# Attention and mixture block on one core: ten maxima ahead of the first scores, transposes of maxima inside a run, the values' bias behind the first split

## The chip, the cores and the metric

The kernel runs on one core of one Trainium2 chip. The metric is the device time of one execution in microseconds; the median of the runs counts. Of the core's engines, TensorE (PE) does the matmuls, VectorE (DVE), ScalarE (ACT) and GpSimd (POOL) the rest, and SyncE (SP) issues the transfers. The engines run beside each other and meet only at semaphores.

## What is computed

The input is x of 2 x 64 x 32 x 32 in f32, that is two batches of 1024 tokens with 64 channels. Cut to what matters:

```python
def _L0_conv_ref(x, ...):                 # softmax attention, 8 heads of 8 channels, then group norm
    q, k, v = proj(Wq, bq), proj(Wk, bk), proj(Wv, bv)
    attn = softmax(einsum('bhnd,bhmd->bhnm', q, k) * scale)
    out  = einsum('bhnm,bhmd->bhnd', attn, v) -> @ Wo.T + bo -> group norm -> + x
x = _L0_conv_ref(x, ...)
t = _to_tokens(x)
t = t + _L1_attn_ref(_ln_t(t), v_matrix, q_matrix)   # 4 layers of 8 linear heads (no softmax)
t = t + _L1_ffn_ref(_ln_t(t), ...)                   # top 2 of 8 experts
```

The change touches only the softmax attention. Everything behind it is the tail.

## The kernel before

**Tiling.** The attention is cut into 16 blocks (batch, pair of heads, half of the queries), each of 8 units (tiles of 128 keys), so there are 128 units. Two units make a run: 64 runs, four to a block. For a unit there are scores (keys on the partitions, 512 queries, for two heads h = 0 and 1: two matmuls of 64 rows), the exp of them on ACT into `probs`, and the values: 8 matmuls that add into one bank over the 8 units of a block. An exp wants the maximum of its query subtracted. So for each block there are also 8 maxima: for 128 queries and one head all 1024 scores are computed once more with the queries on the partitions (two matmuls of 512 columns, `max_half(v, 0)` and `max_half(v, 1)`), and DVE reduces them to one column of `negmax` (L1069). Maximum number v belongs to block v // 8. When a block's eight are out, GpSimd splits them into two parts (for the precision of the f32r matmuls), TensorE turns them into rows, ACT copies these out of PSUM, and they become two more rows of the queries' operand `qop`, so that the scores matmul subtracts the maximum by itself. For blocks 0 and 1 the turning is `rows_of_max` (four matmuls, L464, and two copies by ACT straight into `qop`); for the others it is `maxima_to_rows` (one transpose, L477, called max_t in ST_JOBS), a copy by ACT (L927) and two transfers on SP's queue (`max_rows`, L327).

**Who waits for whom.** The maxima use PSUM banks 0 to 3, two at a time: maximum v waits on `slot_free` until DVE is done with v - 2. Scores, output transposes, max_t and the second batch's projections share a ring of banks 4, 5 and 6 in the order of ST_JOBS, and ACT empties them in the same order. When there are no maxima any more, a unit's two scores take a pair of banks and one exp of 1024 (kind `unit`); these runs are called wide here. Scores of h = 0 and a maximum of h = 1 use different halves of TensorE's rows and run at the same time, which is why the maxima are put between the scores.

**The lead.** Before the first scores, TensorE issues LEAD = 10 maxima. Between them stand the projection for queries and keys of batch 0 in two halves of tokens (`queries_and_keys`, ahead of maxima 2 and 3), the eight tiles of the values' projection, two ahead of each of maxima 4 to 7 (`v_tiles`), and fills behind maxima 7 and 8 (8 small matmuls on zeros each, nothing of the result). The projection goes through ACT and GpSimd (`part`, signalled by `parts0_in` and `parts0`), is stored to DRAM by SP and loaded back as the operands of blocks 2 to 7, ten transfers for each slot. Then comes `rows_of_max(0)`.

**The runs.** `max_jobs(g)` gives the maxima that run g issues: two, but four for the runs in CATCH_UP = (0, 1). So run 0 issues 10 to 13, run 1 14 to 17, run 2 18 and 19, and run 56 the last; units from 114 on are wide. A run with maxima goes: scores, maximum, values(first unit of the run before), maximum, scores, [two more maxima], [rows_of_max(1) in run 2], [output transposes of a block, in run 4k+1], [max_t, also in run 4k+1, for block k+1], values(second unit of the run before). Run 0 has the two projections of batch 1 ahead of its maxima 12 and 13.

**GpSimd's queue** in this part: zeros for the operands, part and split for batch 0, the last copy of q (`rep_pool`, which maximum 8 waits for), the bias of the values (`v_ready`, which values(0) waits for), then for each block the split of its maxima; behind that of block 1 the parts of batch 1 and the zeros of its operands; from block 3 on one `normalize` a block.

## Time and profile before

| | us |
|---|---|
| median of 3 runs | 276.4 |
| lowest, highest | 276.04, 278.12 |
| the profiled execution | 275.98 |
| its span in the profile | 274.2 |

The profile shows one execution. Its span is the time from the first to the last instruction; 1.8 us lie around it. Times in the rows are counted from the span's start. A line number names the line of the kernel that issued an instruction. TensorE's matmuls overlap each other at their ends, so the start of the next instruction is the better measure of what one costs than its own length; the chain view shows the lengths cut in that way.

### The profile page before, as it was taken

How to read it: one execution, taken by the hardware profiler on the slowest of the kernel's cores; microseconds unless marked ns; L12 is line 12 of the kernel's file. 1: busy time of each engine (PE TensorE's matmuls, PEld its weight loads, DVE VectorE, ACT ScalarE, POOL GpSimd, SP SyncE). 2: the span in 40 equal slices, each digit the busy share in tenths (PEclk: the TensorE clock that was granted, in tenths of full speed). 3: DMA queues.
4: the chain of work that ended last, by engine and by line, in shares of the span. 5: the costliest groups of instructions: out<-in, count | busy, mean ns of one | idle time of the engine just before them, and what ended most of it. 6: DMA issues, size and time to landing. Idle time of an engine off the chain costs nothing.

```text
span 274.2 us, 5520 instructions
## 1 busy us (share of the span) xinstructions
PE 253.5 (92%) x2078; PEld 115.3 (42%) x2078; DVE 196.0 (71%) x283; ACT 177.2 (65%) x360; POOL 47.1 (17%) x83
## 2 busy tenths in 40 slices
PE   8999899999999999999999999998986998789895
PEld 6364333333333333333333333332433785558421
DVE  2896566898898898988988989987004662338752
ACT  2725436888897888888888878889792122118720
POOL 7961088110000100000103001000000000000251
PEclk9997757999999999999999999999999999999999
DMA  4046100062122121440100000000000000000002
GB/s 125 0 163 131 22 0 2 15 218 67 40 77 54 29 81 33 99 157 14 68 4 1 1 5 2 1 4 0 5 1 0 2 0 2 0 0 2 1 0 77
DMA packets 6050, 10.30 MB, mean 38 GB/s; under 512 B 2032, under 2 KB 3664, under 8 KB 5896
## 3 DMA queue, kind: packets, MB, share of 16 engines
q1 hardware_dynamic: 6024, 9.95, 12.5%
q8 instruction: 16, 0.26, 0.4%
q14 instruction: 10, 0.08, 0.1%
HBM read 7.10 MB, written 2.62 MB: 35 GB/s over the span
## 4 chain that ended last, share of the span: by engine, by line
PE 77%; DVE 9%; ACT 6%; issue 4%; POOL 1%; DMA 1%; DVEq 0%; SPq 0%; ACTq 0%
PE psum L511 26%; PE psum L418 16%; PE psum L453 15%; ACT probs L915 3%; PE psum L734 3%; PE psum L389 2%; PE psum L643 2%; ACT probs L911 1%; PE psum L477 1%; PE psum L652 1%; DVE negmax L1069 1%; PE psum L715 1%; PE psum L395 1%; PE psum L531 1%; DMA wqk_sb<-in_wqk 1%
## 5 line engine op out<-in xcount | busy, mean ns | idle before, releaser
L1069 DVE TENSOR_REDUCE negmax<-psum 128x1 f32<-128x1024 f32 x128 | 155.2, 1224 | 25.0 <-PE psum L418 22.0
L915 ACT ACTIVATE probs<-psum 128x512 f32<-128x512 f32 x228 | 124.0, 598 | 30.1 <-PE psum L453 24.4
L418 PE MATMUL psum<-kop,qop 64*128 64x512 f32 x256 | 95.1, 460 | 1.7 <-DVE negmax L1069 1.3
L453 PE MATMUL psum<-qop,kop 64*128 64x512 f32 x256 | 90.5, 453 | 0.4 <-DVE negmax L1069 0.3
L511 PE MATMUL psum<-probs,v_aug 128*32 128x256 f32 x1024 | 82.1, 398 | 1.4 <-ACT probs L911 0.3
L418 PEld LDWEIGHTS psum<-kop,qop 64*128 64x128 f32 x256 | 38.6, 192 | 32.9 <-DVE negmax L1069 16.8
L453 PEld LDWEIGHTS psum<-qop,kop 64*128 64x128 f32 x256 | 36.9, 189 | 28.2 <-ACT probs L915 11.1
L511 PEld LDWEIGHTS psum<-probs,v_aug 128*32 128x32 f32 x1024 | 21.4, 109 | 44.8 <-ACT probs L915 30.8
L813 POOL TENSOR_TENSOR attn<-o_tok,rden 128x64 f32<-128x64 f32 x15 | 4.4, 295 | 113.8 <-DVE rden L1060 113.8
L867 POOL TENSOR_TENSOR early<-probs,early 128x512 f32<-128x512 f32 x5 | 6.3, 1269 | 59.6 <-ACT probs L1006 59.5
L521 PE MATMUL psum<-cbf_sb 128*128 128x256 bf16 x124 | 14.8, 272 | 0.0
L911 ACT ACTIVATE probs<-psum 128x1024 f32<-128x1024 f32 x14 | 13.4, 1048 | 1.2 <-PE psum L453 1.2
L521 PEld LDWEIGHTS psum<-cbf_sb 128*128 128x128 bf16 x124 | 12.2, 100 | 1.4
L1060 DVE RECIPROCAL rden<-o_tok 128x8 f32<-128x8 f32 x15 | 2.9, 195 | 11.4 <-ACT o_tok L934 11.4
L1253 DVE TENSOR_TENSOR early<-psum,early 128x512 f32<-128x512 f32 x11 | 7.1, 687 | 4.6 <-PE psum L715 4.6
L734 PE MATMUL psum<-early,expw_sb 128*64 128x512 f32 x32 | 8.2, 610 | 0.5 <-POOL early L867 0.5
L484 PE MATMUL psum<-consts_sb,o_sb 128*128 128x128 f32 x32 | 6.9, 298 | 0.8 <-ACT o_sb L904 0.8
L837 POOL CAST max_part<-negmax 128x8 fp32r<-128x8 f32 x14 | 2.7, 190 | 28.4 <-DVE negmax L1069 28.4
L1006 ACT ACTIVATE probs<-psum 128x512 f32<-128x512 f32 x5 | 3.0, 597 | 6.3 <-PE psum L715 6.2
L477 PE MATMUL psum<-consts_sb,max_part 128*16 128x128 f32 x14 | 3.8, 269 | 3.5 <-ACT probs L915 2.4
L904 ACT ACTIVATE o_sb<-psum 128x256 f32<-128x256 f32 x16 | 6.3, 395 | 0.8 <-PE psum L511 0.8
L389 PE MATMUL psum<-x_sb,wqk_sb 128*128 128x512 f32 x8 | 6.4, 893 | 0.0
(177 smaller groups left out, 199.2 us busy)
## 6 DMA issues: line engine op xcount, KB each, us to landing
parts_scratch<-early SPq DMA_DIRECT2D x4, 512.0 KB, 3.4
qop<-parts_scratch SPq DMA_DIRECT2D x28, 64.0 KB
vt_sb<-in_vt SPq DMA_DIRECT2D x1, 1024.0 KB, 5.0
kop<-parts_scratch SPq DMA_DIRECT2D x14, 64.0 KB
kop<-parts_scratch SPq DMA_DIRECT2D x28, 32.0 KB
x_sb<-in_x SPq DMA_DIRECT2D x2, 256.0 KB, 2.8
q_pair<-in_q_pairs SPq DMA_DIRECT2D x1, 512.0 KB, 3.3
qop<-max_row SPq DMA_DIRECT2D x28, 4.0 KB
```

What stands on the lines that cost most here:

```text
L389: return nc.tensor.matmul(psum[:, bank, :], wqk_sb[:, b, :], x_sb[:, hf * NH:(hf + 1) * NH], start=True, stop=True)
L418: last = nc.tensor.matmul(psum[:, 2 * (v % 2) + c, :], qop[at, b * PP + pp, qh * NH + t * P:qh * NH + (t + 1) * P], kop[at, b * PP + pp, c ...
L453: last = nc.tensor.matmul(psum[:, bank, :], kop[at, b * PP + pp, mt * P:(mt + 1) * P], qop[at, b * PP + pp, qh * NH:(qh + 1) * NH], start= ...
L477: nc.tensor.transpose(psum[0:SPLIT * 2 * HT, bank, 0:P], max_part[:, blk % 2, :, :, :].rearrange("p h s t -> p (h s t)"), ident).then_inc( ...
L484: last = nc.tensor.transpose(psum[:, bank, q * P:(q + 1) * P], o_sb[:, blk % 2, q * P:(q + 1) * P], ident)
L511: last = nc.tensor.matmul(psum[j * VW:(j + 1) * VW, PV_BANK, 0:QB].rearrange("p (x n) -> p x n", x=2), v_aug[:, mt, b, 2 * pp + h, :], pro ...
L521: nc.tensor.matmul(psum[:, bank, 0:WARM_COLS], ident_bf, cbf_sb[:, 1:1 + WARM_COLS // P, :], start=True, stop=True, skip_group_check=True)
L734: nc.tensor.matmul(psum[b * C:(b + 1) * C, MOE_BANKS[c], :], expw_sb[:, k, :], scaled[:, r % SCALED, :], start=False, stop=k == E // 2 - 1 ...
L911: last = nc.scalar.activation(probs[:, n % P_RING, :, :], psum[:, bank:bank + 2, :], ACT.Exp, scale=SCALE)
L915: last = nc.scalar.activation(probs[:, n % P_RING, h, :], psum[:, bank, :], ACT.Exp, scale=SCALE)
L1069: V.tensor_reduce(negmax[:, i, h * HT + t:h * HT + t + 1], psum[:, bank:bank + 2, :].rearrange("p a n -> p (a n)"), AX_X, ALU.max, negate= ...
L1253: V.tensor_tensor(scaled[:, i % SCALED, :], psum[:, GB_BANKS[i % len(GB_BANKS)], :], yt2[:, b, c * NH:(c + 1) * NH], ALU.mult).then_inc(S[ ...
```

## The change

- CATCH_UP is (0,): only run 0 issues four maxima. Run 1 issues 14 and 15, run 2 16 and 17, run 57 the last; units from 116 on are wide.
- In the lead, the first projection stays ahead of maximum 2, together with tile 0 of the values; the second is done in two halves of 256 tokens ahead of maxima 3 and 4; the other tiles stand as V_TILES says (two ahead of maxima 5, 6 and 7, one ahead of 8). There is one fill, behind maximum 8, instead of two.
- max_t of block k+1 moves from behind the scores and output transposes of run 4k+1 to the middle of run 4k+2, behind values(first) and between its two pairs of scores; in a wide run behind its scores.
- The values' bias on GpSimd stands behind the split of block 0 instead of ahead of it.
- The order of the two additional maxima of a doubled run other than run 0 falls away with the run.

```diff
-CATCH_UP = (0, 1)
-FILL_FROM = 7
+CATCH_UP = (0,)
+V_TILES = {2: (0, 1), 5: (1, 3), 6: (3, 5), 7: (5, 7), 8: (7, 8)}
...
-            blk = (g + 3) // RUNS_OF
-            return blk if (g + 3) % RUNS_OF == 0 and DIRECT <= blk <= LAST else None
+            blk = (g + 2) // RUNS_OF
+            return blk if (g + 2) % RUNS_OF == 0 and DIRECT <= blk <= LAST else None
...
             if max_jobs(g):
-                ST_JOBS += [("scores", u, h) for u, h in scores_of(g)]
+                ST_JOBS += [("scores", u, h) for u, h in scores_of(g)[:TOGETHER]]
+                if block_of_rows(g) is not None:
+                    ST_JOBS.append(("max_t", block_of_rows(g), 0))
+                ST_JOBS += [("scores", u, h) for u, h in scores_of(g)[TOGETHER:]]
             else:
                 ST_JOBS += [("unit", u, 0) for u in range(TOGETHER * g, TOGETHER * (g + 1))]
+                if block_of_rows(g) is not None:
+                    ST_JOBS.append(("max_t", block_of_rows(g), 0))
...
-            if block_of_rows(g) is not None:
-                ST_JOBS.append(("max_t", block_of_rows(g), 0))
...
+            def half_queries_and_keys(hf, c):
+
+                return nc.tensor.matmul(psum[:, 4 + hf, c * QB:(c + 1) * QB], wqk_sb[:, 0, :],
+                                        x_sb[:, hf * NH + c * QB:hf * NH + (c + 1) * QB], start=True, stop=True,
+                                        skip_group_check=True)
...
             for v in range(LEAD):
-                if v in (2, 3):
-                    hf = v - 2
-                    pe.wait_ge(S["rep_dve"], hf + 1)
-                    queries_and_keys(0, hf, 4 + hf).then_inc(S["qk_full"], 1)
-                elif 4 <= v < 8:
-                    if v == 4:
-                        pe.wait_ge(S["in_v"], 16)
-                        pe.wait_ge(S["rep_dve"], 3)
-                    elif v == 6:
-                        pe.wait_ge(S["rep_act"], len(CHUNKS) + 1)
-                    v_tiles(2 * (v - 4))
+                if v == 2:
+                    pe.wait_ge(S["rep_dve"], 1)
+                    queries_and_keys(0, 0, 4).then_inc(S["qk_full"], 1)
+                    pe.wait_ge(S["in_v"], 16)
+                    pe.wait_ge(S["rep_dve"], 3)
+                elif v == 3:
+                    half_queries_and_keys(1, 0)
+                elif v == 4:
+                    half_queries_and_keys(1, 1).then_inc(S["qk_full"], 1)
+                elif v == 6:
+                    pe.wait_ge(S["rep_act"], len(CHUNKS) + 1)
+                if v in V_TILES:
+                    v_tiles(*V_TILES[v])
                 for c in range(HALVES):
                     max_half(v, c)
-                if v == FILL_FROM:
+                if v == LEAD - 2:
                     pe.wait_ge(S["parts0_in"], 2 * HALVES)
-                if FILL_FROM <= v < LEAD - 1:
                     fill()
             rows_of_max(0)
...
                     if g:
                         values(TOGETHER * (g - 1))
+                    if block_of_rows(g) is not None:
+                        maxima_to_rows(block_of_rows(g))
                     max_half(jobs[1], 0)
...
                     for u, h in s:
                         scores(u, h)
+                    if block_of_rows(g) is not None:
+                        maxima_to_rows(block_of_rows(g))
...
-                if block_of_rows(g) is not None:
-                    maxima_to_rows(block_of_rows(g))
...
-            pool.wait_ge(S["v_out"], 2)
-            pool.wait_ge(S["in_bv"], 16)
-            v_at = v_aug[:, :, :, :, 0:DH].rearrange("p t b h d -> p t (b h) d")
-            nc.gpsimd.tensor_tensor(v_at, v_at,
...
                 pool.wait_ge(S["max_split"], blk + 1)
+                if blk == 0:
+                    pool.wait_ge(S["v_out"], 2)
+                    pool.wait_ge(S["in_bv"], 16)
+                    v_at = v_aug[:, :, :, :, 0:DH].rearrange("p t b h d -> p t (b h) d")
+                    nc.gpsimd.tensor_tensor(v_at, v_at,
+                                            bv_sb[:].rearrange("p (o h d) -> p o h d", o=1, d=DH).broadcast_to([P, TT, B * H, DH]),
+                                            ALU.add).then_inc(S["v_ready"], 1)
+                    pool.wait_ge(S["v_ready"], 1)
```

## Rows read from the trace of the kernel before

**Rows 1.** The page, busy time, share of the span and instructions of each engine.

```profile
PE 253.5 (92%) x2078; PEld 115.3 (42%) x2078; DVE 196.0 (71%) x283; ACT 177.2 (65%) x360; POOL 47.1 (17%) x83
```

**Rows 2.** Stretches: length, busy us (instructions) by engine, granted clock, DMA share, GB/s.

```profile
24.50:31.20 6.70, 6.70 (x11) 2.43 (x12) 2.33 (x2) 2.66 (x5) 0.00 (x0) 0.50 0.46 78
31.20:34.80 3.60, 2.47 (x17) 0.86 (x14) 3.35 (x3) 2.17 (x4) 0.00 (x0) 0.97 0.00 0
34.80:44.90 10.10, 9.90 (x53) 3.95 (x55) 6.01 (x6) 4.43 (x8) 9.35 (x8) 0.50 0.00 0
...
46.05:189.27 143.22, 139.77 (x1316) 52.35 (x1312) 129.28 (x120) 120.47 (x252) 11.57 (x45) 1.00 0.16 46
189.27:205.50 16.23, 13.72 (x157) 5.76 (x153) 1.16 (x3) 14.50 (x20) 0.98 (x4) 1.00 0.01 3
```

**Rows 3.** Chain that ended last: start us, us, what; the lead.

```profile
1.18 2.45 DMA wqk_sb<-in_wqk
...
11.88 1.06 PE psum L389 x2
...
13.59 0.64 PE psum L395 x4
14.23 0.66 PE psum L418 x2
...
18.85 2.35 POOL v_aug L786
...
23.14 0.74 PE psum L453 x2
```

**Rows 4.** Timeline, lead: start, us, engine, line, operation, count, idle before and releaser.

```profile
13.63 8.86 DVE L1069 TENSOR_REDUCE negmax<-psum 128x1 f32<-128x1024 f32 x7 [0.28 <-PE psum L418]
...
18.73 0.62 PE L471 MATMUL psum<-idle 128*128 128x128 bf16 x8
...
21.80 0.66 PE L464 MATMUL psum<-ident_r,max_wide 128*128 128x128 f32 x4 [0.58 <-POOL max_wide L830]
```

**Rows 5.** Timeline from run 1 to the start of run 5.

```profile
31.45 3.49 DVE L1069 TENSOR_REDUCE negmax<-psum 128x1 f32<-128x1024 f32 x3 [1.93 <-PE psum L418]
...
35.06 0.20 POOL L829 CAST max_wide<-negmax 128x8 fp32r<-128x8 f32 x1 [13.31 <-DVE negmax L1069]
...
37.16 0.79 PE L453 MATMUL psum<-qop,kop 64*128 64x512 f32 x1
...
43.22 3.51 POOL L771 MEMSET kop<- 128x4096 uint32 x1
...
46.05 0.49 PE L453 MATMUL psum<-qop,kop 64*128 64x512 f32 x1
...
48.51 0.50 PE L453 MATMUL psum<-qop,kop 64*128 64x512 f32 x1
```

**Rows 6.** Timeline of a steady run 4k+1, from its start to max_t.

```profile
80.98 0.50 PE L453 MATMUL psum<-qop,kop 64*128 64x512 f32 x1
...
82.07 0.20 POOL L838 TENSOR_TENSOR max_part<-negmax,max_part 128x8 fp32r<-128x8 f32 x1
...
83.02 0.44 PE L484 MATMUL psum<-consts_sb,o_sb 128*128 128x128 f32 x2
...
83.65 0.27 PE L477 MATMUL psum<-consts_sb,max_part 128*16 128x128 f32 x1 [0.19 <-ACT probs L915]
```

**Rows 7.** Timeline of the wide runs, from the last max_t to the last exps.

```profile
192.04 0.27 PE L477 MATMUL psum<-consts_sb,max_part 128*16 128x128 f32 x1 [1.09 <-ACT o_tok L934]
...
192.64 1.27 SPq L327 DMA_DIRECT2D qop<-max_row  x2
...
193.79 5.61 ACT L911 ACTIVATE probs<-psum 128x1024 f32<-128x1024 f32 x6 [1.17 <-PE psum L453]
...
196.57 0.73 PE L453 MATMUL psum<-qop,kop 64*128 64x512 f32 x4
...
201.70 3.77 ACT L911 ACTIVATE probs<-psum 128x1024 f32<-128x1024 f32 x4
```

More of the change, by code:

```diff
@@ L390, in queries_and_keys, with v_tiles @@
                                         start=True, stop=True)
-            def v_tiles(first):
-                c = first // 4
-                for t in range(first, first + 2):
-                    last = nc.tensor.matmul(psum[:, 6 + c, (t % 4) * P:(t % 4 + 1) * P], x_sb[:, t * P:(t + 1) * P],
+            def half_queries_and_keys(hf, c):
+                return nc.tensor.matmul(psum[:, 4 + hf, c * QB:(c + 1) * QB], wqk_sb[:, 0, :],
+                                        x_sb[:, hf * NH + c * QB:hf * NH + (c + 1) * QB], start=True, stop=True,
+                                        skip_group_check=True)
+            def v_tiles(first, end):
+                for t in range(first, end):
+                    last = nc.tensor.matmul(psum[:, 6 + t // 4, (t % 4) * P:(t % 4 + 1) * P], x_sb[:, t * P:(t + 1) * P],
                                             wv_sb[:], start=True, stop=True, skip_group_check=True)
-                if first % 4 == 2:
-                    last.then_inc(S["v_full"], 1)
+                    if t % 4 == 3:
+                        last.then_inc(S["v_full"], 1)
             def max_half(v, c):
@@ L573, in _ @@
                     scores(*s[3])
-                    if g == 0:
-                        for hf, v in enumerate(jobs[2:]):
+                    for hf, v in enumerate(jobs[2:]):
+                        if g == 0:
                             pe.wait_ge(S["in_wqk1"], 16)
                             queries_and_keys(1, hf, st_free(("qk", hf, 0))).then_inc(S["st_full"], 1)
-                            for c in range(HALVES):
-                                max_half(v, c)
-                    else:
                         for c in range(HALVES):
-                            for v in jobs[2:]:
-                                max_half(v, c)
+                            max_half(v, c)
                 else:
```

3 lines of the change are left out of this document (removed).

## Prediction

> **What bounds the kernel now.** I read the page first: TensorE is busy for 92% of the span [rows 1], so it is the first suspect, but a busy share does not tell the pace. So next the stretches, each with its granted clock [rows 2]. From 24.5 to 31.2 us and from 34.8 to 44.9 us the granted clock is 0.50, that is 1.2 instead of 2.4 GHz: 16.8 us at half pace, at the very place where the change works. From 46.05 to 189.27 the clock is 1.00 and TensorE is busy 139.8 of 143.2 us; DVE (129.3) and ACT (120.5) are behind it: the middle is TensorE's. Behind it ACT leads, 14.50 us of 16.23.
>
> Then the chain and the timeline. In the lead TensorE's work stands back to back until it waits for GpSimd [rows 3]: the values' bias takes 2.35 us from 18.85, and the split of the first maxima stands behind it, though its eight maxima are out at 13.63 + 5 x 1.27 = 19.98 (seven reduces in 8.86 [rows 4]; the eighth maximum is the fifth of them). Only the split's end lets rows_of_max(0) go, at 21.80; the first scores start at 23.14. Run 1 is next [rows 5]: it issues four maxima, its TensorE waits for DVE (three reduces in 3.49 us from 31.45; 2.47 us of matmuls in 3.6 us [rows 2]), the clock falls behind it, and run 2 starts only at 37.16. A run at full clock takes 48.51 - 46.05 = 2.46 us; runs 2 and 3 with rows_of_max(1) take 8.89 us, up to 46.05. In the steady part a block of four runs takes 143.22/53 x 4 = 10.81 us. Four times 2.46 is 9.84; the output's transposes take about 0.33 (two of the 0.16 that each of L395's takes), max_t 0.2 of its 0.27, and 0.4 is waiting. Most of it is seen: the output transposes start at 83.02 and are through at 83.35, but max_t starts at 83.65, 0.30 later, since ACT still reads the bank that is next in the ring [rows 6]. The other 0.1 is the wait for o_copied.
>
> **The lead.** The matmuls before rows_of_max(0) stay (two halves of the second projection cost what one whole did) but for one fill: 8 matmuls, 0.62 long, 0.55 to the next instruction. TensorE's contiguous stretch up to 21.22 (21.80 - 0.58 [rows 4]) ends 0.55 earlier, at 20.65. The split now needs maximum 7 alone. In the new order its matmuls end at 18.4 (half a projection less stands ahead of it, and tile 7 behind it), DVE is done at 19.7, and 0.6 us as now (21.80 - 21.20) makes 20.3, before TensorE asks. So rows_of_max(0) starts at 20.6 and the first scores at 21.9, 1.2 us earlier. The bias on GpSimd ends at 22.7; the first to need it is values(0), at 27.8. It hides behind run 0, with 5 us to spare; without that cover it would cost up to 2.35. The second half of the parts reaches GpSimd some 1 us later, and q's last copy, which queues behind it, ends at 18.0, before maximum 8 wants it at 18.7. On SP's queue the store and the operands behind it go 1 us later. Block 2's operands are asked for at 29.8 instead of about 35 us; they are the first of two slots whose ten loads each SP issues from about 21 on, so they should land by 26. I cost all of this at nothing.
>
> **Runs 0 to 3.** If the clock stays up, run 0 goes from 21.9: four scores and maximum 11 until 23.7, then two projections of 1.06 and two maxima of 0.66 [rows 3]: 27.15. Run 1 is an ordinary run, 2.46 and 0.1 for DVE, so run 2 starts at 29.75 instead of 37.16. Runs 2 and 3 with 0.66 for rows_of_max(1) take 5.6: run 4 starts at 35.35 instead of 46.05. That is 10.7 us: 1.2 from the lead, 3 to 4 from two maxima and DVE's waits in run 1, the rest from the clock. Does it stay up? It fell at 24.5 behind 0.58 us of waiting at rows_of_max [rows 4] and lone matmuls on half the rows, and at 34.8 behind a stretch with 1.1 us of idle TensorE [rows 2]. Both go: the wait is gone, the projections move forward into that stretch, and run 1 has no maxima without a scores partner. Against it, the lead loses a fill.
>
> The Trainium skill ("TensorE: Matmul & The Clock Gate", section "A second HAM failure mode: psum-queue depth-cycling") says that frequent short idle times between groups of matmuls are enough to make the gate swing; the fall at 24.5 behind a longest wait of 0.58 us agrees. Its section "HAM oscillation — how this bites in real kernels" blames long waits between bursts; by that alone the clock would never fall in the new kernel. By this second rule the sum stays as it is; by the first, case two of the rivals becomes the likelier one, 265.6.
>
> **A new wait.** GpSimd's work behind the split of block 1 (parts and zeros) runs from 35.06 to 46.73 [rows 5], 11.7 us. Now it starts at 30.8 and ends at 42.5; block 2's split behind it on that queue ends at 43.0. The transpose of these maxima stands in the middle of run 6, at 35.35 + 2 x 2.46 + 0.4 + 1.23 = 41.9. TensorE waits 1.1 us, once, and all its maxima and scores with it.
>
> **The steady part.** max_t moves from behind run 4k+1 into run 4k+2, behind values, and its maxima one run later too. There the ring of three gives it a bank whose scores were read long before, and the scores behind it need exps that end 0.1 us or more ahead. So the 0.30 goes and the 0.2 of work stays. Is the split there? It ends at 82.27, 1.29 into the run that starts at 80.98 [rows 6]; moved by a run whose end holds the output's transposes it is 0.96 into run 4k+2, and TensorE asks at 1.23. 13 blocks x 0.30 = 3.9 us. The other bound is nothing: the 0.30 comes back at another bank. The rows leave later: ACT copies them until 1.85 into the run, SP's second issue starts at 2.5, and run 4k+4 needs them at 5.1, 2.6 later. A landing is not shown. At most it is 3.3 us (the second issue of block 15 starts at 192.64 + 0.64, and the scores at 196.57 don't wait [rows 7]), at least nothing; at 3.3 it costs 0.7 a block. I take the 2.45 of wqk's 64 KB [rows 3], the nearest transfer that the chain shows, so it costs nothing. "DMA: Bandwidth & Descriptors", section "Anatomy of one DMA", in the Trainium skill gives a fixed cost of about 2.0 us; by that there is no wait either.
>
> **The end.** One more run has maxima, one fewer is wide. Run 57 starts at 189.27 - 10.7 + 1.1 - 3.9 = 175.8 and takes 2.46 + 0.4 = 2.9: run 58 at 178.7. The wait of 1.09 us for ACT's copy of the output, which stood here, is gone [rows 7]. But block 15's rows are now copied behind the exps of units 116 and 117, their second issue starts 3.1 into run 58, and they land at about 5.3, where ACT runs dry at 4.3: 1.3 us with the scores' own 0.33. ACT's last twelve exps with two copies took 193.79 to 205.47, 11.7; with 0.4 to start, 0.3 for the row's copy and 1.3 of waiting it is 13.7, to 192.4. The tail behind it is the same work.
>
> **Sum:** 10.7 + 3.9 - 1.1 - 0.4 (16.6 instead of 16.2 from run 57 on) = 13.1 us. The profiled execution took 275.98 (span 274.2 and 1.8 around it), 0.4 under the runs' median of 276.4. 275.98 - 13.1 = 262.9; against the median 263.3.
>
> **Rivals.**
> - *The clock stays up, the sum holds:* 263.3. Chance 0.5.
> - *The clock still falls in runs 0 to 6,* from the thinner lead or the wait of 1.1 us. One low stretch of 6.7 us as now [rows 2] costs 3.4 us, but then GpSimd's wait is hidden: 263.3 + 3.4 - 1.1 = 265.6. Both stretches as now: 16.8/2 - 1.1 = 7.3 on top, 270.6. Chance 0.25.
> - *The moved transpose gives nothing,* its 0.30 coming back as a wait for a bank that ACT holds: 263.3 + 3.9 = 267.2. For it, ACT's share; against it, the ring. Chance 0.12.
> - *The rows land late,* at the bound of 3.3: 0.7 for 13 blocks and 1.0 at the end: 273.4. Chance 0.08.
> - *Slower:* the same place, a landing beyond that. 13.1 us are spent at 0.94 a block of 14, a landing 3.5 us behind the issue; over 1% slower (2.8 us more) from 3.7, at 279. The bound is from the last block, when no other transfer was on the queue; that is all that speaks for it. Chance 0.03. The last 0.02 are for a change that moves nothing: 276.
>
> **How the numbers follow.** The likeliest is 263.3. Below it, the assumed waits of 1.3 at the end and 1.1 at run 6 could be absent: 261. Above, the range takes in one fall of the clock, the 0.30 unmoved, and parts of both: 269.5. Beyond it lie two falls and late rows, under 2 in 10. About 1%, 2.8 us, is what a measurement here can tell from no change. Faster by over 1%: all but the last two cases, 0.95; same 0.02; slower 0.03.
>
> **What would show it.** rows_of_max(0) at about 20.6, the first scores at 21.9; the clock at 1.00 from 20 to 45 us; run 2 at 29.8, run 4 at 35.4; one idle of some 1 us on TensorE ahead of the first max_t; 13 blocks of 10.5 us, with no idle before max_t; no wait for the rows' DMA except ahead of unit 120. It is wrong if the clock row still has its fives there, or if a block stays at 10.8.

## The result, and the profile after

The changed kernel took 264.14 us in the median of four executions (263.63 to 264.78), the kernel before 276.57 beside it (276.04 to 278.12): a ratio of 0.954, with an interval of 0.950 to 0.959. The profiled execution took 264.78, its span is 263.0. The kernel before varies with the clock that it is granted: in the 49 further executions shown below it took 270.6 to 280.05 us, 21 of them over 275, so the 12.4 us of this comparison are not the same thing as what the change is worth in general. That is most of what the experiments are about.

The page of the kernel after: busy time by engine, and TensorE's granted clock in 40 slices.

```profile
span 263.0 us, 5508 instructions
...
PE 245.6 (93%) x2071; PEld 114.5 (44%) x2072; DVE 195.9 (74%) x283; ACT 178.4 (68%) x362; POOL 47.1 (18%) x83
...
PEclk9999999999999999999999999999999999999999
```

TensorE's busy time fell by 7.9 us from the 253.5 of [rows 1], while it issued only seven instructions fewer (the eight of a fill are gone, one more for the second projection in halves). DVE and ACT have nearly the same busy time as before. So most of what TensorE lost is not work but work at half pace: the clock row has no slice below 9 any more, and this answers to the two stretches at 0.50 in [rows 2].

Stretches of the kernel after (length, busy us and instructions by engine, granted clock, DMA share, GB/s), from TensorE's lead to the end of the attention:

```profile
10.90:21.71 10.81, 10.81 (x48) 5.94 (x47) 10.51 (x9) 3.76 (x7) 6.58 (x7) 1.00 0.26 102
...
22.00:29.80 7.80, 7.38 (x34) 3.32 (x35) 6.15 (x6) 5.70 (x10) 1.73 (x1) 1.00 0.56 127
29.80:35.40 5.60, 5.60 (x54) 2.42 (x55) 4.98 (x5) 4.86 (x9) 3.06 (x6) 1.00 0.10 14
35.40:178.70 143.30, 141.26 (x1332) 54.62 (x1333) 131.62 (x122) 123.80 (x258) 18.77 (x47) 1.00 0.16 46
178.70:192.40 13.70, 12.02 (x133) 5.03 (x129) 2.53 (x4) 11.93 (x19) 1.26 (x5) 1.00 0.01 3
```

**The lead.** Everything in this profile stands 1.01 us later than in the one of before: DVE's first reduce starts at 10.88 and not 9.87. The reason is in the chain that ended last; the second row is for the end.

```profile
4.47 2.05 PE psum L386 x2
...
183.95 1.71 DMA qop<-max_row
```

The first f32 matmuls took 2.05 us for two. In the execution of before the same ones took 1.12 (its timeline; the second row is the six matmuls behind them):

```profile
4.38 1.12 PE L383 MATMUL psum<-x_sb,w_rep 128*128 128x512 f32 x2
...
5.71 2.82 PE L383 MATMUL psum<-x_sb,w_rep 128*128 128x512 f32 x6
```

So in the profile after they ran at about half pace, at a place that the change does not touch. The first record of the clock in the trace is its rise, at 6.37 us here and at 3.99 in the profile of before; ahead of that record the view of stretches shows 1.00 all the same. Times of this profile are therefore lowered by 1.0 below where they are set against the prediction.

The timeline of the lead (start, us, engine, line, operation, count, idle time before and its releaser):

```profile
20.82 0.20 POOL L830 CAST max_wide<-negmax 128x8 fp32r<-128x8 f32 x1 [2.02 <-DVE negmax L1078]
...
21.38 2.35 POOL L845 TENSOR_TENSOR v_aug<-v_aug,bv_sb 128x1024 f32<-128x1024 f32 x1
...
21.71 0.66 PE L473 MATMUL psum<-ident_r,max_wide 128*128 128x128 f32 x4
...
23.04 0.73 PE L462 MATMUL psum<-qop,kop 64*128 64x512 f32 x2
```

The split of the first maxima no longer waits for the bias; it is over at 21.30, and rows_of_max(0) starts at 21.71 without the 0.58 of idle time of [rows 4]. Less 1.0 that is 20.7, and the first scores are at 22.0. The bias runs behind the split and holds nobody up.

**Runs 2 to 6.** The timeline of TensorE and GpSimd; the first two rows are the starts of run 2 and run 4.

```profile
30.87 0.49 PE L462 MATMUL psum<-qop,kop 64*128 64x512 f32 x1
...
36.62 0.50 PE L462 MATMUL psum<-qop,kop 64*128 64x512 f32 x1
...
40.17 3.51 POOL L779 MEMSET kop<- 128x4096 uint32 x1
...
43.74 0.19 POOL L838 CAST max_part<-negmax 128x8 fp32r<-128x8 f32 x1
...
44.27 0.28 PE L486 MATMUL psum<-consts_sb,max_part 128*16 128x128 f32 x1 [0.90 <-POOL max_part L839]
```

Run 4 starts at 35.6 on the clock of before, where [rows 5] has 46.05. The price is in the last row: the zeros for the operands occupy GpSimd until 43.7, the split of block 2's maxima stands behind them, and TensorE, done with values at 43.30, waits for it until 44.27, 0.97 us (0.90 in the bracket, the rest is the overlap of matmuls).

**A steady block.** The rows are the starts of two runs 4k+1, a block apart, and between them the output's transposes, the split, max_t and what follows it, and the two transfers of the rows.

```profile
71.80 0.50 PE L462 MATMUL psum<-qop,kop 64*128 64x512 f32 x1
...
73.85 0.44 PE L493 MATMUL psum<-consts_sb,o_sb 128*128 128x128 f32 x2
...
74.22 0.64 PE L520 MATMUL psum<-probs,v_aug 128*32 128x256 f32 x8
...
75.51 0.20 POOL L839 TENSOR_TENSOR max_part<-negmax,max_part 128x8 fp32r<-128x8 f32 x1
...
76.02 0.28 PE L486 MATMUL psum<-consts_sb,max_part 128*16 128x128 f32 x1
76.23 0.49 PE L427 MATMUL psum<-kop,qop 64*128 64x512 f32 x1
...
76.63 1.28 SPq L330 DMA_DIRECT2D qop<-max_row  x2
...
82.39 0.50 PE L462 MATMUL psum<-qop,kop 64*128 64x512 f32 x1
```

A block takes 82.39 - 71.80 = 10.59 us, where the prediction worked out 10.81 for before. max_t has no idle time in front of it; the 0.30 between the output's transposes and max_t in [rows 6] is gone. The split is over at 75.71, 0.3 ahead of max_t.

**The end.** The wide runs: the rows' transfers of the last block, the wait for them, and the last exps.

```profile
183.30 1.26 SPq L330 DMA_DIRECT2D qop<-max_row  x2
...
185.71 0.73 PE L462 MATMUL psum<-qop,kop 64*128 64x512 f32 x4 [1.14 <-DMA qop<-max_row]
...
190.48 3.77 ACT L920 ACTIVATE probs<-psum 128x1024 f32<-128x1024 f32 x4
```

The second transfer is issued at 183.93, and the scores of unit 120 start at 185.71, held by it. The last exps end at 194.25. Run 57 starts at 177.67, so this part takes 16.6 us, as forecast; the wait of 1.09 for the copy of the output in [rows 7] is exchanged for one of 1.14 for the rows.

### The profile page after: what moved, and what is told of

It is laid out like the page before. It is cut to its first block, busy times and chain, and to the rows that moved or that the text cites. A ratio compares the mean times of both kernels' runs of the same rounds, so it can differ in the third digit from the quotient of the medians.

```text
span 263.0 us, 5508 instructions
## 1 busy us (share of the span) xinstructions
PE 245.6 (93%) x2071; PEld 114.5 (44%) x2072; DVE 195.9 (74%) x283; ACT 178.4 (68%) x362; POOL 47.1 (18%) x83
## 4 chain that ended last, share of the span: by engine, by line
PE 76%; DVE 9%; POOL 5%; issue 4%; ACT 3%; DMA 2%; SPq 0%; DVEq 0%; ACTq 0%; POOLq 0%
PE psum L520 23%; PE psum L427 16%; PE psum L462 14%; PE psum L742 3%; PE psum L493 2%; PE psum L651 2%; PE psum L660 1%; POOL qop L779 1%; POOL kop L779 1%; DVE negmax L1078 1%; ACT probs L920 1%; PE psum L392 1%; PE psum L723 1%; PE psum L486 1%; POOL early L857 1%
## 5 line engine op out<-in xcount | busy, mean ns | idle before, releaser
L924 ACT ACTIVATE probs<-psum 128x512 f32<-128x512 f32 x232 | 126.0, 598 | 19.9 <-PE psum L462 15.7
L427 PE MATMUL psum<-kop,qop 64*128 64x512 f32 x256 | 92.7, 444 | 0.6 <-DVE negmax L1078 0.3
L462 PE MATMUL psum<-qop,kop 64*128 64x512 f32 x256 | 89.6, 445 | 1.2 <-DMA qop<-max_row 1.1
L520 PE MATMUL psum<-probs,v_aug 128*32 128x256 f32 x1024 | 80.5, 390 | 1.5 <-ACT probs L920 0.3
L427 PEld LDWEIGHTS psum<-kop,qop 64*128 64x128 f32 x256 | 37.6, 184 | 24.5 <-DVE negmax L1078 13.0
L920 ACT ACTIVATE probs<-psum 128x1024 f32<-128x1024 f32 x12 | 11.6, 1030 | 1.5 <-PE psum L462 1.3
L1015 ACT ACTIVATE probs<-psum 128x512 f32<-128x512 f32 x5 | 3.0, 597 | 6.3 <-PE psum L723 6.2
L889 ACT ACTIVATE early<-psum,rep_cols 128x512 fp32r<-128x512 f32 x4 | 2.9, 775 | 5.2 <-DVE rep_cols L1055 5.1
L779 POOL MEMSET qop<- 128x3072 uint32 (+1 forms) x2 | 6.2, 3086 | 0.1
```

The source lines that it names most:

```text
L427: last = nc.tensor.matmul(psum[:, 2 * (v % 2) + c, :], qop[at, b * PP + pp, qh * NH + t * P:qh * NH + (t + 1) * P], kop[at, b * PP + pp, c ...
L462: last = nc.tensor.matmul(psum[:, bank, :], kop[at, b * PP + pp, mt * P:(mt + 1) * P], qop[at, b * PP + pp, qh * NH:(qh + 1) * NH], start= ...
L520: last = nc.tensor.matmul(psum[j * VW:(j + 1) * VW, PV_BANK, 0:QB].rearrange("p (x n) -> p x n", x=2), v_aug[:, mt, b, 2 * pp + h, :], pro ...
L779: nc.gpsimd.memset(op[:, slots, :].bitcast(U32), 0).then_inc(S["padded"], 1)
L920: last = nc.scalar.activation(probs[:, n % P_RING, :, :], psum[:, bank:bank + 2, :], ACT.Exp, scale=SCALE)
L924: last = nc.scalar.activation(probs[:, n % P_RING, h, :], psum[:, bank, :], ACT.Exp, scale=SCALE)
```

## The experiments

**Two theories** stood against each other after this. *The schedule*: each part of the change takes its waits away, and the clock only follows, since in the old kernel it falls behind idle time on TensorE (the prediction's account). *The clock*: most of the gain is that the new order keeps the clock up, and whether it falls is not a matter of idle time. All kernels of one group ran on one chip beside the kernel before.

### The bias alone

The kernel before, with the bias of the values behind the split of block 0 and nothing else:

```diff
-            pool.wait_ge(S["v_out"], 2)
...
-            pool.wait_ge(S["v_ready"], 1)
             chain = [3]
...
                 pool.wait_ge(S["max_split"], blk + 1)
+                if blk == 0:
+                    pool.wait_ge(S["v_out"], 2)
...
+                    pool.wait_ge(S["v_ready"], 1)
```

> The kernel before with one edit: the values' bias stands behind the split of block 0 on GpSimd. Theory (as in the prediction, two causes for the early gain): rows_of_max(0) no longer waits 0.58 us, TensorE goes on at 21.2, first scores 0.6 us earlier; run 1 still issues four maxima and its clock dip stays; the first dip (24.5) may go, since the wait ahead of it is gone. Time 275.9 if both dips stay (-0.6), 272.5 to 273.5 if the first one goes (-0.6 and half of 6.7 us, less what DVE takes back in run 1). Rival: the bias alone carries the early gain: run 4 at 36 instead of 46, time 266 to 268.

Measured: 273.31 us in the median of ten (269.9 to 280.01), ratio 0.995 (0.989 to 1.000) to 25 executions of before with a median of 273.7 (270.68 to 279.29). Both kernels fall into groups by the clock of their whole span: before has nine at 270.7 to 271.2 with a clock of 0.992, and seven at 276.3 and more with 0.951 to 0.968; bias_only has four at 269.9 to 270.5 with 0.993, and four at 276.9 and more with 0.957. Among those with a high clock the part is worth 0.8 us, near the 0.58 that it removes.

The profiled execution is one of the long ones, 277.06. First its rows_of_max(0), from the timeline:

```profile
21.08 0.66 PE L464 MATMUL psum<-ident_r,max_wide 128*128 128x128 f32 x4
```

Then its stretches, ahead of rows_of_max(0) and behind 24.7 us:

```profile
10.00:21.08 11.08, 11.06 (x53) 5.87 (x53) 10.50 (x9) 3.72 (x6) 7.54 (x8) 1.00 0.28 106
...
24.70:45.00 20.30, 19.41 (x80) 7.39 (x78) 11.03 (x10) 8.35 (x15) 9.79 (x8) 0.50 0.14 26
```

The wait is gone, TensorE was busy for 11.06 of 11.08 us before it, and the clock falls all the same, at the same place, and stays down for 20.3 us. So the wait of 0.58 us was not what made it fall in [rows 2].

### One doubled run alone

```diff
-CATCH_UP = (0, 1)
+CATCH_UP = (0,)
```

> The kernel before with CATCH_UP = (0,) alone: maxima one run later, max_t stays at the end of run 4k+1. Theory: the split of a block then ends about 3.75 us into run 4k+1 while TensorE asks for it at 2.4, so each of 13 blocks waits 1.4 us instead of 0.3: +14 us, against 4 to 5 won in run 1: about 286, more (to 295) if the clock falls behind these waits. The moved transposes are then what the one doubled run needs. Rival: the doubled run is the gain and the transposes only go along: 268 to 270.

Measured: 305.39 us (305.21 to 308.8, four executions), ratio 1.124 (1.112 to 1.136): 34.5 us more than the best group of before (270.9), and worse than expected. TensorE's wait for the split, once in each block (in total, times, longest), and one place of it in the timeline:

```profile
PE psum L477 <- POOL max_part L838: 22.0, 14, 2.7
```

```profile
111.45 0.33 PE L477 MATMUL psum<-consts_sb,max_part 128*16 128x128 f32 x1 [1.48 <-POOL max_part L838]
...
111.71 1.08 PE L511 MATMUL psum<-probs,v_aug 128*32 128x256 f32 x8
```

Maxima that come one run later are split one run later, and a max_t at the end of run 4k+1 asks before the split is there: 22.0 us of idle TensorE in 14 places. Behind it the eight matmuls of values take 1.08 instead of 0.64 us: the clock has gone to its lower level, and it does so again and again (the whole span has 0.926). The waits are 22.0 us where the profile of before has 2.4, that is 19.6 of the excess. A clock of 0.926 over 303.5 us is 45 us at half pace, which can cost up to 22, and run 1 gives some 3 back; the parts were not taken apart further. The doubled run may only go together with the move of max_t.

The same profile shows one thing more, ahead of its first fall at 46.7 us:

```profile
24.00:46.00 22.00, 18.82 (x143) 7.76 (x143) 16.41 (x14) 16.16 (x32) 12.15 (x11) 1.00 0.17 31
```

This kernel has the old lead and the wait of 0.58 us at rows_of_max(0), at 22.34, and its TensorE is idle for 3.2 of these 22 us, and yet the clock stays at 1.00 in this execution.

### The kernel before, its idle places filled

Eight small matmuls on zeros ahead of rows_of_max(0), and 4, 5 and 12 of them in run 1 ahead of three of its maxima, in unused columns of the values' bank. In this first form they begin a new sum in that bank, and the result is off by 0.028, presumably because the values' sum of the first unit of block 0 is lost; in the second form, further below, it is not.

```diff
+            fill()
             rows_of_max(0)
...
+                    if g == 1:
+                        fill_beside(4)
                     max_half(jobs[1], 0)
...
                             for v in jobs[2:]:
+                                if c == 0:
+                                    fill_beside(5 if v == jobs[2] else 12)
                                 max_half(v, c)
```

> The kernel before with more small matmuls on zeros in the places where TensorE waits: 8 ahead of rows_of_max(0), and in run 1 4 ahead of maximum 15, 5 ahead of 16 and 12 ahead of 17 (into unused columns of the values' bank). No order and no dependency changes, so it measures the clock by itself. Theory: the granted clock stays at 1.00 from 20 to 45 us; run 0's two projections take 1.06 instead of 2.0 each, runs 2 and 3 take 5.6 instead of 8.9 us; 270 to 271.5. Rival 1: the waits, not the clock, are the time: 276.5 or a little more. Rival 2: the fills do not hold the clock: rows at 0.50 remain, 276 to 277.

Measured: 272.37 us (269.68 to 274.33, ten executions), ratio 0.999 (0.993 to 1.005), and none above 275, where 12 of the 25 of before were. Its profile (272.17 us), one stretch and the start of run 4:

```profile
14.00:52.00 38.00, 37.41 (x278) 17.93 (x278) 32.54 (x28) 23.89 (x45) 18.37 (x17) 1.00 0.24 69
```

```profile
40.77 0.49 PE L453 MATMUL psum<-qop,kop 64*128 64x512 f32 x1
```

The clock stays at 1.00 through both places where it fell, and run 4 starts 6.3 us earlier than in the profile of before (40.77, less 1.05 by which this profile is late, against 46.05). That is what the low clock had cost there. With a full clock the old schedule is still 39.7 - 35.6 = 4.1 us behind the changed one at run 4: this is the lead and run 1. The median lies 0.9 us above the range expected; the profiled execution has 1.05 us of it from its slow start.

### The changed kernel with the bias back ahead of the split

```diff
+            pool.wait_ge(S["v_out"], 2)
...
+            pool.wait_ge(S["v_ready"], 1)
             chain = [3]
...
-                if blk == 0:
-                    pool.wait_ge(S["v_out"], 2)
...
-                    pool.wait_ge(S["v_ready"], 1)
```

> The changed kernel with the bias back ahead of the first split. Theory: the bias can start only when the second half of the values is copied (about 20.0), so the split ends near 22.8 and rows_of_max(0) starts 1.1 us later: 265.2 with the clock at 1.00 throughout; if the wait of 1.1 us makes the clock fall once, another 2 to 3.4: 267 to 268.5. Rival: the cover is elsewhere and the bias costs nothing: 264.1.

Measured: 270.6 us (269.28 to 271.17, ten executions), 6.5 above the changed kernel, more than either figure expected. The wait, from the timeline, and the stretch with the low clock:

```profile
22.96 1.11 PE L473 MATMUL psum<-ident_r,max_wide 128*128 128x128 f32 x4 [1.78 <-POOL max_wide L838]
```

```profile
22.80:36.30 13.50, 13.34 (x40) 6.33 (x44) 6.03 (x5) 6.05 (x11) 0.11 (x1) 0.51 0.31 69
```

The wait is 1.78 us here and not 0.58, since the new order has the projections' tiles later and TensorE at rows_of_max earlier, while the bias takes its 2.33 us as before. Behind it 13.5 us run at a clock of 0.51, in all ten executions (their spans have 0.973 to 0.98). Run 2 starts at 36.79 where the changed kernel has 30.87, and this profile's lead is 0.6 earlier (DVE's first reduce at 10.26), so run 2 is 6.5 us late: 1.8 of waiting, and 4.7 of low clock. That is the whole difference. So this part, worth 0.8 us by itself in the old kernel, carries 6.5 in the new one.

### The second group: the lead, run 1, and the filled kernel without its fault

The changed kernel again first:

> The changed kernel as it is, beside the kernel before on the same chip. The kernel before spread from 270.7 to 279.3 us in the last job, with granted clocks of the whole span from 0.992 down to 0.951. Theory: the changed kernel has no place left where the clock falls, so it stays within 1.5 us around 264, and against the kernel before in its executions at clock 0.99 it wins 6.5 us, against the others up to 15. Rival: its clock falls in some executions too, and it spreads by 3 us and more.

Measured: 264.31 us (263.59, 263.87, 264.76, 266.66), ratio 0.974 (0.965 to 0.983) to 13 executions of before with a median of 272.81. The one of 266.66 is the profiled one. Its timeline has the reason, at the replicas of the projection:

```profile
6.87 4.57 PE L386 MATMUL psum<-x_sb,w_rep 128*128 128x512 f32 x6
```

The six took 2.82 us in the profile of before. Here they ran at about half pace; the first record of the clock in this trace is its rise at 10.40 us, and ahead of it the view shows 1.00.

Run 1 doubled again, with everything else as changed (run 56 is then the last with maxima):

```diff
-CATCH_UP = (0,)
+CATCH_UP = (0, 1)
...
+                        for c in range(HALVES):
+                            for v in jobs[2:]:
+                                max_half(v, c)
```

> The changed kernel with CATCH_UP = (0, 1) and the old order of the four maxima of run 1; lead, bias and max_t as changed. Theory: run 1 waits for DVE some 3 us, as in the kernel before; the clock falls behind it in part of the executions; at the end one wide run more and one ordinary run less give 0.4 back: 266.5 at clock 1.00, 268 to 271 where it falls. Rival: four maxima in run 1 are harmless once the lead is shorter: 264.

Measured: 266.31, 266.45, 269.16 and 271.01 us, with clocks of 0.993, 0.992, 0.981 and 0.974; ratio 0.984 (0.973 to 0.994). One of the waits for DVE in run 1, in the profile of the execution of 266.45, and the stretch behind them:

```profile
31.08 0.72 PE L427 MATMUL psum<-kop,qop 64*128 64x512 f32 x3 [0.64 <-DVE negmax L1082]
```

```profile
32.00:35.30 3.30, 3.30 (x22) 1.13 (x16) 3.12 (x3) 1.08 (x2) 3.08 (x4) 0.51 0.00 0
```

Counted from DVE's first reduce, so without the start, this profile is 3.9 us behind the changed kernel's at run 4 and 2.5 at its end: the rest comes back because the wait at the first max_t is gone and one run more is wide. The expected time at a clock of 1.00 was not seen, since even the best executions have a short low stretch; it is part of the 2.5.

The old order of the lead, with its two fills, in the changed kernel (the `for v in range(LEAD)` loop of before; the tiles two ahead of each of maxima 4 to 7):

```diff
-                if v == 2:
...
+                if v in (2, 3):
+                    hf = v - 2
+                    pe.wait_ge(S["rep_dve"], hf + 1)
+                    queries_and_keys(0, hf, 4 + hf).then_inc(S["qk_full"], 1)
...
-                if v == LEAD - 2:
+                if v == FILL_FROM:
                     pe.wait_ge(S["parts0_in"], 2 * HALVES)
+                if FILL_FROM <= v < LEAD - 1:
                     fill()
```

> The changed kernel with the lead's old order (two whole projections ahead of maxima 2 and 3, two tiles ahead of each of 4 to 7, two fills). Theory: maximum 7 ends later by half a projection less one tile, and one more fill stands in the contiguous stretch: rows_of_max(0) 0.55 us later, nothing else: 264.7, clock 1.00. Rival: the lead's new order is what keeps the clock up: a stretch at 0.50 and 267 or more.

Measured: 265.15, 266.8, 266.95 and 270.4 us with clocks of 0.998, 0.987, 0.987 and 0.981; ratio 0.980 (0.972 to 0.988). Stretches of the profile (270.4 us):

```profile
13.00:23.99 10.99, 10.97 (x52) 5.77 (x53) 10.40 (x9) 3.72 (x6) 5.01 (x7) 1.00 0.29 107
...
27.00:37.80 10.80, 10.72 (x37) 3.84 (x36) 5.61 (x5) 4.52 (x9) 0.15 (x1) 0.53 0.25 54
```

TensorE was busy for 10.97 of 10.99 us ahead of rows_of_max(0), which it reached without a wait and with one fill more than the changed kernel, and the clock fell at about 27.0. The changed kernel's own stretch is the first one above, 10.81 of 10.81, and there it stays up. The two hardly differ in how busy TensorE is, only in what it does when.

The schedule part is small. rows_of_max(0) starts at 23.99, that is 11.28 behind DVE's first reduce (12.71), where the changed kernel has 10.83: 0.45 us, near the 0.55 expected. At its end this execution is 3.8 us behind the changed kernel, counted in the same way, so about 3.4 are the low clock. The other 2.8 of its 270.4 us are a slow start, and for the executions without a profile the two cannot be told apart.

A rival is that the start decides whether the clock falls later. Two pairs of profiles speak against it. after_again started as late as this one (first reduce at 12.77) and its clock never fell; after_rows_at_end, further below, started as early as bias_only (9.72 and 9.80), and only bias_only's fell.

The filled kernel of before without its fault, the small matmuls adding to zero columns (`start=False`):

> The kernel before with small matmuls on zeros where TensorE waits, as in before_kept_busy, but adding into the unused columns instead of starting a new sum there (in before_kept_busy that start wiped the sum of unit 0's values; here the whole computation is kept). Theory: the same clock and time as there, 269.7 to 274.3, median 272.4, with run 2 at about 33.5 to 34.5 and run 4 at about 40 to 41: the executions above 275 of the kernel before are gone. Rival: the fills only shift the low stretches: the kernel before's spread to 279 is back.

Measured: 272.29 us in the median of ten (seven at 271.51 to 272.76, two at 274.0 and 274.11, one at 278.07), ratio 1.004 (1.000 to 1.008). With both forms, 1 execution of 20 is above 275, of before 21 of 49. So with the fills the clock stays up more often. What they cost isn't shown: this median is 1.3 us over the best group of before, but its profiled execution (272.16) starts 0.87 us later than the profile of before, and counted from the first reduce rows_of_max(0) stands at 11.93 in both. In its profile the clock falls elsewhere, behind the wait for ACT's copy of the output ahead of the last max_t:

```profile
186.00:191.00 5.00, 4.27 (x37) 1.68 (x37) 0.20 (x1) 2.50 (x5) 0.29 (x1) 0.66 0.03 7
```

### The third group: the place of max_t, and a version beyond

The changed kernel with max_t at the end of run 4k+2 instead of its middle (and ST_JOBS in that order):

```diff
-                    if block_of_rows(g) is not None:
-                        maxima_to_rows(block_of_rows(g))
                     max_half(jobs[1], 0)
...
                             max_half(v, c)
+                    if block_of_rows(g) is not None:
+                        maxima_to_rows(block_of_rows(g))
```

> The changed kernel with max_t at the end of run 4k+2 (behind all four scores) instead of in its middle. In the changed kernel the row's second transfer starts 2.5 us into run 4k+2, lands in 1.8 us (block 15: 183.93 to 185.71), and run 4k+4 asks 0.9 us later. Theory: at the end of run 4k+2 the ring gives max_t a bank that ACT has left, so no wait at max_t, but ACT copies it behind two more exps, 1.2 us later, and TensorE waits 0.2 to 0.4 us for the transfer at the start of every block: 264.2 + 13 x 0.3 = 268, the idle put down to DMA. Rival: it is the bank that the middle place saves, then 0.3 us at max_t in each block, put down to ACT: also 268, but told apart by the releaser. Second rival: both have slack: 264.2.

Measured: 268.09 us (267.13 to 268.2, four executions, all with a clock of 0.999 or 1.0), ratio 0.982 (0.976 to 0.988). The waits of TensorE for the rows (in total, times, longest), and one of them in the timeline with the transfers that it waits for:

```profile
PE psum L461 <- DMA qop<-max_row: 4.3, 13, 1.1
```

```profile
87.57 1.31 SPq L329 DMA_DIRECT2D qop<-max_row  x2
...
90.03 0.49 PE L461 MATMUL psum<-qop,kop 64*128 64x512 f32 x1 [0.27 <-DMA qop<-max_row]
```

At this place the landing is on the path in each of 13 waits. This is the prediction's rival of late rows made to happen. It costs 3.5 us counted from the first reduce to the end of the profile (255.6 for 252.1); the medians differ by 268.09 - 263.89 = 4.2, starts included. The second issue goes at about 88.2 and the scores at 90.03, 1.8 us; the chain gives the landing alone 1.71 to 1.74 in twelve blocks and 2.15 in one.

The changed kernel once more, for the comparison:

> The changed kernel once more, as the measure for the two runs beside it: 263.6 to 264.8, with an execution in four up to 2.8 us longer where the first matmuls of the kernel run at half pace.

Measured: 263.89 us (263.65 to 264.3, six executions, clocks 0.998 to 1.0), ratio 0.967 (0.963 to 0.972).

A version beyond both: the last quarter of GpSimd's zeros behind block 2's split instead of ahead of it, and max_t of the first wide run between its two units instead of behind them:

```diff
                 if blk == DIRECT:
...
+                    pad(1)
                 for hf in range(HALVES if blk == 1 else 0):
...
-                    if hf == HALVES - 1:
-                        pad(1)
...
                     for u, h in s:
+                        if u % TOGETHER and not h and block_of_rows(g) is not None:
+                            maxima_to_rows(block_of_rows(g))
                         scores(u, h)
-                    if block_of_rows(g) is not None:
-                        maxima_to_rows(block_of_rows(g))
```

> The changed kernel with two more edits: the zeros of batch 1's operands on GpSimd behind the split of block 2 instead of block 1's, and in the first wide run max_t between the scores of its two units instead of behind both. Theory: TensorE's wait of 0.97 us ahead of the first max_t goes (the split then ends when its maxima do), and block 15's rows reach SP one exp (0.93 us) earlier, so the wait of 1.14 us ahead of unit 120 shrinks to 0.2 to 0.4: 262.4 to 262.8 beside 264.2, clock 1.00. Rival: the 7 us of zeros delay something behind them (the split of block 3, the ones rows of batch 1), or max_t now waits for the split ahead of unit 117 and ACT runs dry: 264 or more.

Measured: 262.74 us (262.08 to 262.29 three times with a clock of 1.0, 263.19 to 263.64 three times with 0.993), ratio 0.963 (0.958 to 0.968), so 1.2 us less than the changed kernel in the median and 1.5 among the executions with a clock of 1.0. The first max_t, then the last one with its transfers and unit 120:

```profile
42.89 0.28 PE L487 MATMUL psum<-consts_sb,max_part 128*16 128x128 f32 x1
...
180.18 0.28 PE L487 MATMUL psum<-consts_sb,max_part 128*16 128x128 f32 x1 [0.48 <-POOL max_part L840]
...
180.94 1.26 SPq L331 DMA_DIRECT2D qop<-max_row  x2
...
183.48 0.73 PE L463 MATMUL psum<-qop,kop 64*128 64x512 f32 x4
```

The wait of 0.97 at the first max_t is gone. At the end one of 0.48 for the split takes the place of the 1.14 for the rows. This profile is one of the three with 0.993: unit 120 starts 1.8 us earlier than in the changed kernel (both from the first reduce, 10.44 and 10.88), but the span ends only 0.8 earlier. The clock, expected at 1.00, falls behind the wide runs:

```profile
190.00:200.00 10.00, 7.65 (x55) 3.83 (x52) 3.09 (x8) 4.08 (x6) 0.00 (x0) 0.84 0.00 0
```

## Why the prediction was right, and where it was not

**The time.** 263.3 was forecast, 264.14 measured, and 263.9 is the median of the third group. The likeliest case came, the clock up and the sum nearly whole.

**Positions without the start.** The start differs by up to 3 us between executions, so the profiles are best compared from DVE's first reduce (at 9.87 before, 10.88 after). Starts in us from there:

| profile | rows_of_max(0) | run 2 | run 4 | run 57 | end of span |
|---|---|---|---|---|---|
| before | 11.93 | 27.29 | 36.18 | 179.40 | 264.3 |
| bias_only | 11.28 | 27.01 | 36.07 | 179.26 | 265.5 |
| before_filled | 11.93 | 23.42 | 29.83 | 173.22 | 259.5 |
| one_doubled_only | 11.94 | 21.11 | 26.87 | 206.00 | 293.1 |
| after | 10.83 | 20.00 | 25.74 | 166.79 | 252.1 |
| after_again | 10.84 | 20.01 | 25.76 | 166.73 | 252.1 |
| after_bias_back | 12.70 | 26.53 | 32.29 | 173.11 | 258.5 |
| after_lead_back | 11.28 | 24.50 | 30.45 | 170.57 | 255.9 |
| after_doubled_back | 10.84 | 22.67 | 29.65 | 169.65 | 254.6 |
| after_rows_at_end | 10.83 | 19.99 | 25.75 | 170.28 | 255.6 |

**The lead** came as worked out: rows_of_max(0) at 20.7 for 20.65, the first scores at 22.0 for 21.9. By the table its 1.10 us are 0.65 from the bias (11.93 to 11.28, bias_only) and 0.45 from the new order with one fill fewer (11.28 in after_lead_back, 10.83 after). The bias is hidden behind run 0, as said.

**Runs 0 to 3.** Run 2 at 29.9 for 29.75, run 4 at 35.6 for 35.35. The 0.26 that run 4 is late lie in run 3 for about half: its last scores start 0.14 after the maximum's that they should go with (35.49 and 35.63 in the timeline), behind ACT's two copies for block 1. The 10.7 us of this step divide into 6.3 of clock (before_kept_busy), and 4.1 of lead and run 1, with 0.3 not reached. Of the 4.1, run 1 is 3.0, since one_doubled_only, whose clock is full up to there, has run 4 at 26.87 and before_filled at 29.83. The prediction had 4.2 to 5.2 for both, with 3 to 4 for run 1, so this was sound at its lower end. (Its 27.15 and 2.56 make 29.71, not 29.75; nothing hangs on it.)

**The clock.** That it would stay up was right, but the reason given for the first fall was wrong. "It fell at 24.5 behind 0.58 us of waiting at rows_of_max" does not stand: bias_only and after_lead_back have no wait there and fall within 4 us of rows_of_max(0). "Against it, the lead loses a fill" was no danger either: with the old lead and its two fills the clock falls in three executions of four. The Trainium skill, in the section that the prediction quoted ("TensorE: Matmul & The Clock Gate", section "A second HAM failure mode: psum-queue depth-cycling"), has frequent short idle times between groups of matmuls make the gate swing; the traces with 11.06 of 11.08 and 10.97 of 10.99 us busy ahead of the fall do not agree with that as the cause here. For the fall in run 1, idle time on TensorE is argued and not shown: after_doubled_back brings both the waits for DVE and a low stretch back, and in one_doubled_only the matmuls are slow behind a wait of 1.48 us, but the same profile holds 1.00 through 3.2 idle us in 22.

bias_only and after_lead_back share the old lead: the projections of batch 0 as two matmuls ahead of maxima 2 and 3, the tiles of the values earlier, and one fill more. That putting it back matters is shown (the changed kernel has clocks of 0.998 to 1.0 in all 14 executions, after_lead_back 0.981 to 0.987 in three of four); why is not, nor whether it is the order or the fill. The old lead doesn't make the clock fall each time either: it held in the profile of one_doubled_only, wait and all, and the old kernel does both from one execution to the next. That stays open. What is shown is that each of three things, put back into the changed kernel, lowers the clock: the wait at rows_of_max in ten executions of ten, the old lead in three of four, the four maxima of run 1 in four of four (0.993 and less).

**What was not examined.** The prediction took the two low stretches of one profiled execution for the kernel's own, in every execution. They are not: 9 of 25 executions of before in the first group have a clock of 0.992 and take 270.9. Against these, the change brings 270.9 - 263.9 = 7.0 us: by the terms 4.1 for lead and run 1, 3.1 for the steady part, less 1.0 at GpSimd and 0.4 at the end, that is 5.8. The rest of about 1.2 would be the clock: in the profile of before_filled, with 0.992 too, the low stretch lies at the end of the attention, and from run 57 to the end it takes 86.3 us where before took 84.9. No execution of before with 0.992 was profiled, so that it falls there as well is an inference. Against executions with both stretches it is 13 and more. The forecast of 263.3 depends on this only for its comparison, since the changed kernel hardly varies; its range would have been as good with either.

**The new wait.** 0.97 for 1.1, at the place forecast. The step was right and its size 0.13 too large.

**The steady part** is the term that was mis-sized: 10.59 a block for 10.5. From the start of run 4 to that of run 57 it is 177.67 - 36.62 - 0.97 = 140.1 us for 53 runs, 10.57 a block, so 0.24 gained and not 0.30, 3.1 us for 3.9. The bank wait is wholly gone, as forecast; but the output's transposes cost 0.37 (73.85 to 74.22) and not 0.33, and max_t 0.21, and the wait for o_copied stays. The saving of 0.30 was added to a block whose parts were rounded to a tenth.

**The landing.** 2.45 was taken, the copy of the weights being the nearest transfer. 1.7 to 1.8 us was measured: 1.71 in the chain of after, and 1.71 to 1.74 in that of after_rows_at_end, with one of 2.15. The bound of 3.3 was far off, so the case of late rows was never near. The Trainium skill ("DMA: Bandwidth & Descriptors", section "Anatomy of one DMA") gives about 2.0 us as the fixed cost of a transfer on another path; the row is 0.2 to 0.3 below that. That the row's place decides anyway is shown by after_rows_at_end, where half a run later makes 13 waits of it.

**The end.** 16.6 us as forecast, by errors that cancel, so by luck in part: the wait ahead of unit 120 is 1.14 for 1.3. The rows are issued 3.3 into run 58 for 3.1 and land at 5.0 for 5.3. The forecast had a slip as well: an issue at 3.1 and the landing of 2.45 that it took make 5.55 and not 5.3, which would have put 0.25 more on the wait.

**Sum.** Less 1.0 for its slow start, the profiled execution took 263.8. Against 262.9 that is 0.9 more: 0.8 of the steady part and 0.26 of run 4, less 0.13 at GpSimd.

## What to carry to other kernels

Look at the granted clock of several executions before you count a low stretch as the kernel's own: here one kernel took 270.6 to 280 us, and a change can be worth 7 or 13 us by which of them it is set against. Move a producer and its consumer together: the maxima one run later cost 34.5 us where max_t stayed, and gained where it moved too. When a long piece of work on a side engine can go before or behind a short one that TensorE waits for, the short one goes first, at both places here (the bias and the zeros).

## What the runs showed of the hardware

- The start of an execution varies by up to 3 us: the first two f32 matmuls took 2.05 us in one execution and 1.12 in another, the next six 4.57 and 2.82. The trace's first record of the clock is its rise, at 6.37, 3.99 and 10.40 us in these three profiles (after, before, after_again), and ahead of it the view shows 1.00.
- The clock falls from 1.00 to 0.50 behind 11.06 of 11.08 us of busy TensorE (bias_only), so a full TensorE alone does not keep it up; and it stayed at 1.00 through 22 us with 3.2 of them idle (one_doubled_only). Once down it stayed for 20.3 us of stretch in bias_only, for 13.5 in after_bias_back and for some 3.3 in after_doubled_back.
- A transfer of the rows within SBUF lands 1.71 to 1.74 us after its issue in the chain of after and in twelve of the 13 blocks of after_rows_at_end, and after 2.15 us in one.
- With small matmuls that start a new sum in unused columns of the values' bank the kernel's result is off by 0.028 (before_kept_busy); with ones that add to zero columns, and nothing else changed, it is not (before_filled). That it is the running sum of the first unit that goes is inferred from where they stand.
